# Where the squares behind the query and key norms are computed: ScalarE activations or GpSimd products

## What is computed

```python
q, k, v = (split_heads(x @ W.T) for W in (Wq, Wk, Wv))
q_norm_sq = jnp.sum(q * q, axis=-1, keepdims=True)
k_norm_sq = jnp.sum(k * k, axis=-1)[:, :, None, :]
diff_sq = jnp.maximum(q_norm_sq + k_norm_sq - 2.0 * qk, 0.0)
denom = jnp.maximum((1.0 - q_norm_sq) * (1.0 - k_norm_sq), 1e-06)
cosh_arg = jnp.maximum(1.0 + 2.0 * diff_sq / denom, 1.0)
attn = jax.nn.softmax(-jnp.arccosh(cosh_arg), axis=-1)
out = (attn @ v) @ Wo.T
linear = xn @ int4(kernel) + bias + (xn @ a) @ b
```

## Time and profile before

| | |
|---|---|
| median of 3 runs | 2472.44 us (2471.17 to 2472.47) |
| the profiled execution: its own time | 2470.88 us |
| its span, first to last instruction | 2469.2 us |
| mean granted TensorE clock | 0.99 of full |
| prologue (8 tiles, weights) | about the first 165 us |
| attention periods with a projection (p = 0 to 55) | to about 2150 us |

### The profile page before, as it was taken

How to read it: one execution, slowest core, us unless ns; L and a number is a source line. 1 busy time by engine, 2 the same in 40 slices (tenths; PEclk the granted TensorE clock), 3 DMA queues, 4 the chain that set the end, 5 groups by cost and what they waited for, 6 DMA issues and landing times. The chain is left out here.

```text
span 2469.2 us, 45016 instructions
## 1 busy us (share of the span) xinstructions
PE 2262.4 (92%) x17416; PEld 818.8 (33%) x17416; DVE 2031.2 (82%) x2780; ACT 2147.2 (87%) x2022; POOL 90.6 (4%) x75
## 2 busy tenths in 40 slices
PE   4889999999999999999999999999999999977774
PEld 1433333333333333333333333333333333322221
DVE  7778888888888888888888888888888888876662
ACT  2249999999999999999999999999999999999990
POOL 1000000000000000000000000000000000000000
PEclk8999999999999999999999999999999999999997
DMA  3551342533545443354534435454333544343314
GB/s 131 135 161 49 107 107 78 137 109 108 141 124 141 110 118 105 112 141 124 141 92 134 112 107 141 124 141 121 108 105 112 141 116 133 103 119 89 89 41 125
DMA packets 357000, 285.82 MB, mean 116 GB/s; under 512 B 81296, under 2 KB 296464, under 8 KB 356784
## 3 DMA queue, kind: packets, MB, share of 16 engines
q1 hardware_dynamic: 356784, 282.91, 41.4%
HBM read 160.30 MB, written 121.63 MB: 114 GB/s over the span
## 5 line engine op out<-in xcount | busy, mean ns | idle before, releaser
L414 ACT ACTIVATE root<-pU 128x1024 f32<-128x1024 f32 x1024 | 1030.9, 1028 | 52.5 <-PE pU L189 44.0
L418 ACT ACTIVATE root<-root 128x2048 f32<-128x2048 f32 x512 | 983.8, 1922 | 40.7 <-DVE root L651 40.0
L651 DVE TENSOR_SCALAR root<-root 128x2048 f32<-128x2048 f32 x512 | 625.0, 1221 | 105.1 <-ACT root L414 104.8
L189 PE MATMUL pU<-QS,KS 100*128 100x512 f16 x2048 | 615.5, 382 | 70.9 <-ACT root L414 64.8
L656 DVE TENSOR_TENSOR root<-root 128x2048 f32<-128x2048 f32 x256 | 585.6, 2288 | 46.9 <-PE pO L199 27.5
L199 PE MATMUL pO<-root,VX 128*32 128x512 f32 x4096 | 547.6, 604 | 51.0 <-ACT o_s L424 48.6
L189 PEld LDWEIGHTS pU<-QS,KS 100*128 100x128 f16 x2048 | 145.4, 97 | 603.9 <-ACT root L414 291.9
L213 PE MATMUL pZ<-root,ones 128*32 128x512 f32 x2048 | 269.8, 593 | 1.0 <-DVE root L656 1.0
L257 PE MATMUL pM<-Wqh,xT 128*128 128x512 f16 x512 | 174.5, 385 | 5.3 <-DVE feat_ql L610 5.3
L257 PE MATMUL pM<-Wvh,xT 128*128 128x512 f16 x512 | 173.4, 382 | 2.6 <-ACT qk L439 2.6
L257 PE MATMUL pM<-Wkh,xT 128*128 128x512 f16 x512 | 171.8, 379 | 0.0
(11 more groups left out here) (106 smaller groups left out, 2144.9 us busy)
## 6 DMA issues: line engine op xcount, KB each, us to landing
v_d<-v_o SPq DMA_DIRECT2D x64, 264.0 KB, 2.1
k_d<-kx SPq DMA_DIRECT2D x64, 264.0 KB, 2.2
KT<-k_d SPq DMA_DIRECT2D x64, 264.0 KB
VX<-v_d SPq DMA_DIRECT2D x64, 264.0 KB
xt<-in_x SPq DMA_DIRECT2D x32, 512.0 KB, 4.2
res_d<-f_o SPq DMA_DIRECT2D x64, 256.0 KB, 3.8
QS<-qh_d SPq DMA_DIRECT2D x128, 128.0 KB
KS<-kh_d SPq DMA_DIRECT2D x128, 128.0 KB
```

What stands on the lines that cost most here:

```text
L189: mm = pe.matmul(pU[:, col:col + HALF], KS[i][:, h, j * P:(j + 1) * P], QS[i][:, h, half * HALF:(half + 1) * HALF], start=True, stop=True)
L414: act.activation(root[:, q % RING, cols], pU[:, cols], ACT.Square).then_inc(squared, 1)
L418: act.activation(root[:, q % RING, :], root[:, q % RING, :], ACT.Sqrt).then_inc(rooted, 1)
L651: v.tensor_scalar(root[:, q % RING, :], root[:, q % RING, :], CS * CS, CS * CS, ALU.max, ALU.subtract).then_inc(clamped, 1)
```

## The change

For tiles 8 to 63 ACT no longer squares; `take_qk` ends after the copy. POOL does both squares of the tile as a product of qk with itself, into the same `sqr`, with the same semaphores towards DVE. The order of POOL's list becomes: queries' squares, keys' squares, bias of tile n; for n from 8 to 63. The first 8 tiles stay as they were.

```diff
@@ take_qk (ACT)
                 act.activation(qk[:, s, :], pM[b][:, :], ACT.Copy, scale=scale[:, IQ + s:IQ + s + 1]).then_inc(taken["qk"[s]], 1)
+                if n >= LEAD:
+                    return
                 act.wait_ge(taken["qk"[s]], n + 1)
                 if 2 * n + s:
                     act.wait_ge(summed, 2 * n + s)
@@ gpsimd_program (POOL)
+            def square_qk(n, s):
+                g.wait_ge(taken["qk"[s]], n + 1)
+                g.wait_ge(summed, 2 * n + s)
+                g.tensor_tensor(sqr[:, :], qk[:, s, :], qk[:, s, :], ALU.mult).then_inc(squared_qk, 1)
+
@@ the list of POOL
-            for n in range(LEAD + 2):
+            for n in range(LEAD):
                 add_bias(n)
-            for p in range(PERIODS):
-                if p + LEAD + 2 < NT:
-                    add_bias(p + LEAD + 2)
+            for n in range(LEAD, NT):
+                square_qk(n, 0)
+                square_qk(n, 1)
+                add_bias(n)
```

## The result

| | before | after |
|---|---|---|
| median | 2472.45 us (4 runs) | 2439.43 us (4 runs, 2438.24 to 2440.09) |
| the profiled execution | 2470.88 us | 2440.09 us |
| its span | 2469.2 us | 2438.0 us |
| ratio after / before | | 0.9867 [0.985, 0.9884] |

33 us faster, where 37 were forecast (2436); the range of 2413 to 2454 holds it. In the changed kernel the lines behind the edit are numbered higher: the clamp is L653 (before L651), the last line of the division L639 (L637), the pair addition L658 (L656), the norm sum L565 (L563), POOL's bias addition L770 (L768), its product L775.

A forecast was written before the change was run, and what follows sets the result against it. ACT was taken to bound periods 1 to 7 and PE those from 8 on; 28 us from the even periods plus 9 from the first eight gave 37 us less, 2436 us as a median, range 2413 to 2454.

The forecast's parts named there:

- The event: Even periods from 8: ACT's keys' square waits 1.59 us for DVE's sum, delaying copy L424; PE loses 1.79 us.
- Periods 0 to 7: First eight periods: ACT is the bound, its relief gains 1.1 us a period, 9 us in all, bounds 6 to 10.
- Periods 8 to 55: PE is full; only even periods gain, 1.17 us of PE's 1.79 us stall each, 24 times, 28 us.
- the late clamp before slot 8: Even periods: POOL makes DVE's clamp end 0.8 to 0.94 us later, limiting PE's gain to 1.17 us a pair.
- The order assumed: Even period: DVE's clamp goes before POOL's queries' product; later SBUF work on DVE or the sum is 1.13 to 1.28 us later.
- rival 1: Even periods: POOL goes ahead of the first clamp, delaying it 1.13 to 1.28 us; gain 33 us, 2439 us; chance 0.25.
- a wait of some 18 us of PE's L199 for `o_s`: Sign that POOL runs ahead of the clamp: PE's wait for the copy falls from 41.7 us to about 18.
- rival 2: No contention that counts: all of PE's stall goes, gain 51 to 57 us, 2415 to 2421 us; chance 0.22.
- DVE's idle time of 0.34 us: Even period, in front of L651: DVE can give up this idle time, reducing the clamp's delay to 0.8 to 0.94 us.
- Rival 3: Slower: norms arrive late on DVE in even periods; with 4 us lost, 27 us slower, 2499 us; chance 0.07.
- products last over 2 us in the rows: Sign on POOL's products, forecast at about 1.28 us, that would show the prediction wrong.

The follow-up runs named there:

- second buffer: Kernel before, all squares on ACT, with separate buffers for the queries' and the keys' squares: 2438.28 us, ratio 0.9856.
- queries only: Against the kernel before, only the queries' square goes to POOL, the keys' square stays on ACT: 2507.58 us, ratio 1.0147.
- an interval across zero in the experiment: Against the kernel before, products on POOL for tiles 8 to 15 alone: 2471.24 us, ratio 0.9993 [0.9984, 1.0002].
- the experiment with POOL's extra wait: Changed kernel, but POOL's queries' product waits until DVE has done the clamp of slot 2: 2427.16 us, ratio 0.9813 against the kernel before.

## Why the prediction was right, and where not

**The event.** That PE loses 1.79 us once per even period because ACT's keys' square waits for DVE's norm sum held in every run: the stall went with the wait (second buffer), stayed with it (queries only), and went wholly when the keys' square alone moved.

**Periods 0 to 7: wrong.** The step was "ACT is the bound, and ACT's 1.3 us fits under PE's 1.6 us": 9 us forecast, 0.1 measured in the time lines, 1.2 with an interval across zero in the experiment. Both numbers were right as means of a period. But the 1.6 us lie from slot 8 on and the squares in 2 and 4, and ACT cannot carry a lead from the one to the other, since its squares of the distances follow PE's matmuls with two halves of pU between them. It could have been read before: PE's time line says in which slots PE waits.

**Periods 8 to 55: right in size, by the wrong term.** 28 us were forecast from a gain limited to 1.17 us per pair by the late clamp before slot 8; 32.4 us came, 1.35 per pair. The limit did not act in the changed kernel, where ACT's wait at this place is 0.6 us and PE starts no later for it (12.20 us from the same value sum to L189). The order assumed (DVE's clamp first) did not occur either: POOL went first, as rival 1 had it. Rival 1 gave 0.9 to 1.07 us per pair, and its error was one of size: a product of 1.04 us in place of 1.28 holds the clamp 0.84 us, where 1.13 to 1.28 stood. Its sign, a wait of some 18 us of PE's L199 for `o_s`, did not come either: PE meets the late ACT earlier, at the weight loads that wait for the keys' copy (10.6 us), so the sign by itself would have spoken for the forecast or rival 2. With the order assumed, in the experiment with POOL's extra wait, the kernel gains 1.86 us a pair, not 1.17. The chain of that limit was right and its size was not: counted from the start of the split L637 (L639), the clamp before slot 8 comes at 15.78 us, before at 15.47, so DVE was 0.3 us late, not 0.8 to 0.94. The product holds DVE for 0.76 us instead of 1.13 to 1.28, and DVE's idle time of 0.34 us takes up its part, as forecast.

**The total.** 28 + 9 = 37 against 33: of the 9 us that did not come, the 4 us too few in the second stretch hide about half. The number was better than its steps. That rival 1's total, 2439, is the measured one is luck of the same kind: 24 us where 32.4 came, and the same 9 us that did not.

**The lock.** That DVE yields to a running POOL instruction was read from one 128x32 row; the changed kernel shows it for the clamp (2.06 for 1.22 us), and the other way round: products that become ready under a pair addition last 2.00 us in 23 of the 24 odd periods from 9 on. The chance of 0.25 for rival 1 was too low for a product that is ready before the clamp. The Trainium skill (SBUF — State Buffer, Who interferes with whom) says that the one that issues first holds the shared pair for its whole instruction. These rows agree: the product starts 0.18 us ahead of the clamp and the clamp lasts 0.84 us longer. With the clamp held 0.84 us ACT comes to its copy L424 1.38 us earlier than before (7.23 in place of 8.61), so the gain is about 1.4 us per pair where the full stall is 1.79.

**The slower side.** Rival 3 did not occur; the norm sums never waited for POOL. One of its signs did come: "products last over 2 us in the rows". Of the 112 products 32 lasted 2.0 us or more, the longest 3.04, and this did no harm, since no sum waited for them: the sign was badly chosen. But the experiment with the queries alone shows how near it was: the same product in front of the same clamp, with the old wait left in place, is 35 us slower than before.

## What to carry to other kernels

When two engines are both near full, compare them slot by slot, not by a period's mean: relief on the one is worth only what the other waits for at that place. Before work is moved to a slower engine, ask whether the loss is the work or a wait on a single buffer; here a second buffer of 2 KB a partition gives the whole gain of the change, with all squares left on ACT. And where POOL works beside DVE's SBUF instructions, choose by a semaphore which of the two goes first: one wait was worth 12 us.

## What the runs showed of the hardware

- A POOL tensor_tensor of 128x512 f32 takes 1.04 us with the same tile as both operands (a product into another tile, an addition in place) and 1.28 us with two tiles (an addition in place).
- POOL's product held DVE's clamp (tensor_scalar, 128x2048 f32) by 0.84 us and a 128x2 tensor_tensor by 0.76 us; a DVE tensor_tensor of 128x2048 in front held the product by about 1 us (2.00 for 1.04), and the clamp behind the product was held 0.70 us (1.92 for 1.22).
- PE waits of 2.22 us were followed by a fall of the granted clock in 10 of 23 periods; a fall cost 1.65 us. Waits of 1.79 us, 24 times, were followed by none. In the tail longest waits of 1.9 in place of 1.5 us went with a mean clock of 0.91 in place of 1.00, and with 7 us in the last eight periods (one trace each; that the waits caused the fall is not shown).
